# A recommender kernel's first chunk: first cross layer tile by tile in fp32, with the next tiles' attention groups between

## The chip, the cores and the metric

One core of one Trainium2 chip. The metric is the device time of one execution in microseconds (us). The kernel before took 2104.42 us, the median of three runs (2103.35 to 2104.58).

## What is computed

A recommender model for 2048 samples. Each sample has a target (an item embedding plus a projected image embedding), a history of 50 items, and two category fields.

```python
x = concat([t, seq_emb, t - seq_emb, t * seq_emb])          # 50 history items, 128 wide each
scores = (relu(x @ aw1 + ab1) @ aw2 + ab2)[..., 0]
weights = softmax(where(item_seq == 0, -1e9, scores))
hist_feat = einsum('bs,bsd->bd', weights, seq_emb)
sparse = stack([like_feat, view_feat, item_id_feat, item_img_feat, hist_feat])   # 5 x 128
se = sparse * w[:, :, None]                                  # gate from the fields' means
p = [vids[:, i] * se[:, j] for i in range(4) for j in range(i + 1, 5)]
dnn_in = concat([se, p])                                     # 15 x 128 = 1920
for i in range(2):
    xc = dnn_in * (xc @ cross_K[i] + cross_bias[i]) + xc
h = gelu(ln(xc @ w1 + b1)); h = gelu(ln(h @ w2 + b2)); return sigmoid(h @ w3 + b3)
```

## The kernel before

The samples are 16 tiles of 128, in four chunks of four tiles. Samples lie along the free axis in the cross layers: the 1920 features are 15 blocks (FEATS) of 128 partitions.

**A tile's attention** goes in five *groups* of ten history items. GpSimd gathers the items by indirect DMA (L445), ten a group and three more for a tile's features. For a group TensorE transposes the ten blocks (`transposes10`, L503; in the opening two halves, L496 and L509), ScalarE copies them to SBUF (`copy_eT10`), VectorE multiplies them by the target (`times_target`, L1116), TensorE computes the hidden layer (`hidden`, L528 and L532), VectorE takes the maximum (`hidden_max`, L1130), TensorE makes the scores (`score`, L539), VectorE does four small softmax operations (`softmax_max`, L1138 to L1144), ScalarE takes exponentials and weighs the ten blocks (`exps`, `weigh`, L829), and VectorE sums them (`history`, L1164 and L1167). Once a tile, VectorE prepares the target (`head_aim`, from L1093) and its negative (`head_neg`, L1108 and L1109), finishes the history and the gate (`tail_fold` from L1172, `tail_gate_apply`), and multiplies the pairs of fields (`tail_pairs`, L1199).

**The plan** (`make_plan`) sets the order by hand. A `Step` names what every engine issues in it: `grp` (transposes and `times_target`) at step k, `open` (`hidden`, `hidden_max`, `score`) at k + 1, `summed` (softmax, `weigh`, `history`) at k + 2. Each engine walks the same steps and takes its own part, in a fixed order. An opening of 28 steps prepares the first chunk's four tiles, with a group in nearly every step and no cross layer. A last group of its last tile is split (TAPER).

**A chunk** then is 30 steps, 15 output blocks in each of two cross layers, and a stage for `w1`. A step is three `products` calls of five feature blocks. Weights come from HBM into a ring of six (`raw`), and each is split into a high and a low part in fp32r (`w_hi` on ScalarE, `w_lo` on VectorE); activations likewise (`x_hi`, `x_lo`). Each block then takes three matmuls of 512 columns (L586 to L588). The attention groups of the next chunk's tiles lie inside these steps: groups at steps 1 to 5, 7 to 11, 13 to 17 and 19 to 23. In a step TensorE issues products 0, `hidden`, `transposes10`, products 1, products 2, `score`. VectorE's order in a step is, in short:

```python
if p.summed: softmax_max(*p.summed)
unit(c, 3 * k); if prev: x_scale(*prev)      # the previous output block
if p.open: hidden_max(p.open[0])
if p.summed: history(*p.summed)
unit(c, 3 * k + 1); if prev: x_lo(*prev)
if p.pair is not None: tail_pairs()
if p.grp: times_target(p.grp[0])
unit(c, 3 * k + 2)                           # then tail_gate_apply, tail_fold, head_aim
```

Two PSUM banks alternate between output blocks: products 0 of a step waits on `bank_free`, which VectorE gives after `x_scale` of the block before last. Loading the first `raw` blocks does not wait; later ones wait on `w_free`.

## Time and profile before

| | |
|---|---|
| median of the runs | 2104.42 us |
| profiled execution's own time | 2105.34 us |
| its span | 2103.0 us |
| PE / DVE / ACT / POOL busy | 92% / 64% / 43% / 43% |
| opening (to the first product of chunk 0) | 327.4 us |
| chunk 0, layer 0 | 327.4 to 539.4 us |
| moved by DMA | 220.27 MB |

The span is the time from the first to the last recorded instruction, and the execution's own time has 2.3 us more around it. A busy share of PE counts a matmul until its result has drained, so overlapping ones run closer together than their durations: the distance from one start to the next is what a matmul costs in a stream. An fp32 matmul shows as two records (x8 for four matmuls), a transpose or an fp32r matmul as one.

### The profile page before, as it was taken

To read this page: it belongs to the slowest core of one execution; us is meant where nothing else is said; L and a number is where in the kernel's file an instruction comes from. 1 tells how busy PE (TensorE), PEld (TensorE's weight loads), DVE (VectorE), ACT (ScalarE), POOL (GpSimd) and SP (SyncE) were. 2 spreads that over 40 slices of the span, in tenths; PEclk is the share of its full clock that TensorE was granted. 3 is DMA by queue.
4 is the path that set the end of the run, shared out by engine and by line. 5 is a ranking of instruction groups with operands and counts; after the bars stand their busy time and mean duration, and the time that the engine had idled before them with its cause. 6 is when DMAs were issued, how large, how long until landed. Compare 5 with 4: busy or idle time off the path is not lost. (4 is left out here: it accounts for less than half of the span.)

```text
span 2103.0 us, 32483 instructions
## 1 busy us (share of the span) xinstructions
PE 1936.4 (92%) x9608; PEld 1522.7 (72%) x9608; DVE 1337.0 (64%) x2248; ACT 903.0 (43%) x1927; POOL 893.9 (43%) x854
## 2 busy tenths in 40 slices
PE   1766658999999999999999999999999999999997
PEld 1444436778777887777777887777777888888886
DVE  4555555677778756667778755667778654445553
ACT  1443442545445244664544335654445243322234
POOL 7777777667566401657557302647550000000000
PEclk7666568999999999999999999999999999999998
DMA  5112113334344452334434452334432343333320
GB/s 164 50 49 53 48 52 98 104 111 137 115 121 121 137 174 79 96 90 142 117 111 132 129 182 71 100 96 140 116 106 88 116 167 126 93 96 97 98 68 1
DMA packets 99675, 220.27 MB, mean 105 GB/s; under 512 B 21792, under 2 KB 27184, under 8 KB 99376
## 3 DMA queue, kind: packets, MB, share of 16 engines
q1 hardware_dynamic: 63072, 136.90, 21.5%
q0 software_dynamic: 27136, 55.63, 10.4%
q10 hardware_dynamic: 9296, 25.70, 3.3%
q8 instruction: 79, 1.29, 0.3%
q14 instruction: 92, 0.75, 0.1%
HBM read 205.29 MB, written 12.85 MB: 104 GB/s over the span
## 5 line engine op out<-in xcount | busy, mean ns | idle before, releaser
L445 POOL DMA_INDIRECT e<-in_item_table,idx_all x800 | 843.7, 1055 | 649.4 <-POOLq L467 416.1
L870 ACT ACTIVATE Wh<-raw 128x640 fp32r<-128x640 f32 (+1 forms) x411 | 293.8, 723 | 508.9 <-ACTq L869 506.5
L1225 DVE TENSOR_TENSOR Wl<-raw,Wh 128x640 fp32r<-128x640 f32 (+1 forms) x411 | 331.9, 808 | 278.1 <-DVEq L1224 276.1
L586 PE MATMUL psum<-X0h,Wh 128*128 128x512 f32 x900 | 361.3, 401 | 1.3 <-PEq L584 1.3
L586 PE MATMUL psum<-X1h,Wh 128*128 128x512 f32 x900 | 357.1, 397 | 0.0
L587 PE MATMUL psum<-X0l,Wh 128*128 128x512 f32 x900 | 351.4, 390 | 0.0
L588 PE MATMUL psum<-X0h,Wl 128*128 128x512 f32 x900 | 351.1, 390 | 0.0
L587 PE MATMUL psum<-X1l,Wh 128*128 128x512 f32 x900 | 350.9, 390 | 0.0
L588 PE MATMUL psum<-X1h,Wl 128*128 128x512 f32 x900 | 350.4, 389 | 0.0
L829 ACT ACTIVATE e<-e,pw 128x128 f32<-128x128 f32 x800 | 242.8, 388 | 15.3 <-ACTq L142 15.3
L586 PEld LDWEIGHTS psum<-X0h,Wh 128*128 128x128 f32 x900 | 169.4, 188 | 36.5 <-issue 3.4
L588 PEld LDWEIGHTS psum<-X0h,Wl 128*128 128x128 f32 x900 | 169.1, 188 | 36.6
L588 PEld LDWEIGHTS psum<-X1h,Wl 128*128 128x128 f32 x900 | 169.0, 188 | 36.0
L586 PEld LDWEIGHTS psum<-X1h,Wh 128*128 128x128 f32 x900 | 169.1, 188 | 34.6 <-issue 1.0
L587 PEld LDWEIGHTS psum<-X1l,Wh 128*128 128x128 f32 x900 | 169.2, 188 | 32.8
L587 PEld LDWEIGHTS psum<-X0l,Wh 128*128 128x128 f32 x900 | 169.6, 188 | 32.1
L1164 DVE TENSOR_REDUCE hist<-e 128x128 f32<-128x1280 f32 (+1 forms) x65 | 156.6, 2408 | 52.9 <-DVEq L1162 52.9
L528 PE MATMUL psum<-eT,A 128*64 128x512 f32 (+2 forms) x640 | 138.5, 513 | 18.3 <-PEq L522 17.9
L1116 DVE TENSOR_TENSOR teT<-eT,tT 128x1280 f32<-128x1280 f32 x79 | 117.5, 1487 | 43.4 <-DVEq L1114 43.3
L539 PEld LDWEIGHTS psum<-cols,hidT 128*128 128x128 f32 x800 | 115.0, 217 | 35.5 <-issue 31.6
L539 PE MATMUL psum<-cols,hidT 128*128 128x2 f32 x800 | 110.2, 263 | 28.7 <-PEq L537 28.7
L532 PE MATMUL psum<-teT,A 128*64 128x512 f32 (+2 forms) x640 | 135.5, 503 | 0.0
(159 smaller groups left out, 2168.2 us busy)
## 6 DMA issues: line engine op xcount, KB each, us to landing
raw<-in_cross_K SPq DMA_DIRECT2D x360, 320.0 KB
raw<-in_w SPq DMA_DIRECT2D x51, 256.0 KB
e<-in_item_table,idx_all POOLq DMA_INDIRECT x800, 2.5
dnn_scratch<-dn ACTq DMA_DIRECT2D x12, 960.0 KB
x1f<-dnn_scratch ACTq DMA_DIRECT2D x3, 2048.0 KB, 9.8
x1f<-dnn_scratch ACTq DMA_DIRECT2D x3, 1792.0 KB, 15.6
e<-in_w SPq DMA_DIRECT2D x9, 256.0 KB, 4.8
dn<-in_embT SPq DMA_DIRECT2D x1, 1024.0 KB, 5.4
```

The costliest lines, as they stand in the source:

```text
L445: nc.gpsimd.indirect_dma_start(out=dst, out_offset=None, in_=table, in_offset=bass.IndirectOffsetOnAxis(ap=idx_all[:, t, s:s + 1], axis=0) ...
L528: last = mm(hsum[u * HID:(u + 1) * HID, a:b], A12[:], eT[:, u, a:b], start=True, stop=False)
L532: last = mm(hsum[u * HID:(u + 1) * HID, a:b], A3[:], teT[:, u, a:b], start=False, stop=True)
L539: last = mm(to[:, 2 * s:2 * s + 2], hidT[:, s * P:(s + 1) * P], col("aw2h", 0, 2), start=True, stop=True)
L586: m0 = mm(out, wh, Xh[:, 0:T, k, :], start=(k == 0), stop=False)
L587: m1 = mm(out, wh, Xl[:, 0:T, k, :], start=False, stop=False)
L588: m2 = mm(out, wl, Xh[:, 0:T, k, :], start=False, stop=(k == FEATS - 1))
L829: last = af(x, x, ACT.Copy, scale=pw[:, g % 2, s:s + 1])
L870: af(Wh[:, split_slot(w), 0:n], raw[:, rs, 0:n], ACT.Copy).then_inc(hi_done, 1)
L1116: v.tensor_tensor(teT[:].rearrange("p u (s b) -> p (u s) b", b=P), eT[:].rearrange("p u (s b) -> p (u s) b", b=P), tT[:, par:par + 1, :].t ...
L1164: done(v.tensor_reduce(hist[:] if g else acc[:, par, :], x, AX.X, ALU.add))
L1225: v.tensor_tensor(Wl[:, rs, 0:n], raw[:, rs, 0:n], Wh[:, slot, 0:n].bitcast(F32), ALU.subtract).then_inc(lo_done, 1)
```

## The change

Only chunk 0 and what leads up to it change. The opening now prepares one tile (OPEN = 1, 13 steps). Then come 45 *early* steps: three passes of 15 output blocks, one for each of tiles 0, 1 and 2, each computing layer 0 of its tile alone in plain fp32 (`solo_products`: one fp32 matmul of 128 columns for a block, no split of weights or activations). Tile 3's pass is the first 15 steps of chunk 0. In place of 675 fp32r matmuls of 512 columns there are 900 fp32 matmuls of 128 columns. Of the 15 output blocks' weights, those of even n (8 of them, 24 loads of 320 KB) are kept in SBUF (`kept`, where X1h and X0h lie later); the odd ones are streamed again in each pass. `solo_scale` is a VectorE operation on 128 x 128 in place of one on 128 x 512. TensorE waits for all kept blocks before the first pass.

The groups of tiles 1 to 4 are placed by SPREAD, counted from the end of the opening; tiles 5 to 7 come at steps 8, 14 and 20 and the four after each. The fields of tiles 0 to 3 are written straight into x0f, so that splitting them in the opening (`tail_hi`, `tail_lo`) goes, and in layer 1 of chunk 0 the sum X0h + X0l (`x_sum`) goes too. Blocks 0 to 13 of the first layer's result are split for layer 1 in pairs at steps 8 to 14 of tile 3's pass (HALVES). The first weight unit of layer 1 is split at step 14.

```diff
+OPEN = 1
+LAST = OPEN - 1
+PASSES = TILES[0] - 1
+KEPT = 8
+HALVES = {FULL + 2 + q: (2 * q, 2 * q + 1) for q in range(FEATS // 2)}
+SPREAD = ((-2, 0, 1, 3, 5), (8, 11, 14, 17, 20), (23, 26, 29, 32, 35), (38, 41, 44, 47, 50))
 GROUP_STEPS = {
     4: [[1 + 6 * j + g for g in range(NG)] for j in range(4)],
+    0: [[s + g for g in range(NG)] for s in (8, 14, 20)],
...
-    open_steps = lead + sum(len(groups(t)) for t in range(TILES[0])) + 4
+    open_steps = lead + sum(len(groups(t)) for t in range(OPEN)) + 4
+    early_steps = open_steps + PASSES * FEATS
+    plan += [Step(0, k, a) for a in range(PASSES) for k in range(FEATS)]
...
+            for b in range(KEPT * UNITS):
+                if b > 1:
+                    sp.wait_ge(kept_landed[b % 2], b // 2 * DMA)
+                n, kg = divmod(b, UNITS)
+                sp.dma_start(kept[:, n, kg * KG:(kg + 1) * KG, :].rearrange("p f b -> p (f b)"), kx_d[2 * n * UNITS + kg]).then_inc(kept_landed[b % 2], DMA)
...
+            def solo_products(a, n, kg):
+                out = xps[:, bank(a, n), 0:P]
+                if kg == 0:
+                    pe.wait_ge(bank_free, 1).then_inc(bank_free, -1)
...
+                    last = mm(out, block(i), x0f[:, a, k, :], start=(k == 0), stop=(k == FEATS - 1))
...
+            for i in range(2):
+                pe.wait_ge(kept_landed[i], KEPT * UNITS // 2 * DMA)
+            for p in early:
+                step(p)
...
+            def solo_scale(a, n):
+                dve.wait_ge(mm_done, 1).then_inc(mm_done, -1)
+                v.scalar_tensor_tensor(out=x1f[:, a, n, :], in0=xps[:, bank(a, n), 0:P], scalar=col("cb", n), in1=x0f[:, a, n, :],
+                                       op0=ALU.add, op1=ALU.mult).then_inc(scaled, 1)
...
+                if p.last:
+                    solo_scale(*p.last)
+                elif p.prev:
+                    x_scale(*p.prev)
```

VectorE before, at the end of layer 0 of chunk 0: from a group's softmax (L1138) in one step to the next group's `times_target` (L1116, output teT).

```order
L1138 SCALAR_TENSOR_TENSOR sc<-psum,tiny,keep 128x10 [waits score_ready]
L1141 TENSOR_TENSOR sc<-sc,mbias 128x10 [waits dve_done]
L1142 TENSOR_REDUCE tiny<-sc 128x1 [waits dve_done]
L1144 TENSOR_SCALAR nmax<-tiny 128x1 [waits dve_done]
L1225 TENSOR_TENSOR Wl<-raw,Wh 128x640 [waits hi_done]
L1253 SCALAR_TENSOR_TENSOR x1f<-psum,cols,x1f 128x4x128 [waits sum_done,mm_done]
L1130 TENSOR_TENSOR hidT<-psum,negT 128x640 [waits lo_done,scaled,h_ready]
L1149 COPY rsum<-gsum 128x1 [waits p_ready]
L1164 TENSOR_REDUCE acc<-e 128x128 [waits dve_done,weighed]
L1225 TENSOR_TENSOR Wl<-raw,Wh 128x640 [waits dve_done,hi_done]
L1271 TENSOR_TENSOR X1l<-x1f,X1h 128x4x128 [waits xhi_done]
L1116 TENSOR_TENSOR teT<-eT,tT 128x1280 [waits lo_done,eT_ready]
```

VectorE in the change, in the second pass over the spaced groups, from the softmax of one group (L1204) to `hidden_max` of the next (L1196); L1302 is `solo_scale`.

```order
L1204 SCALAR_TENSOR_TENSOR sc<-psum,tiny,keep 128x10 [waits score_ready]
L1207 TENSOR_TENSOR sc<-sc,mbias 128x10 [waits dve_done]
L1208 TENSOR_REDUCE tiny<-sc 128x1 [waits dve_done]
L1210 TENSOR_SCALAR nmax<-tiny,nmax 128x1 [waits dve_done]
L1302 SCALAR_TENSOR_TENSOR x1f<-psum,cols,x0f 128x128 [waits mm_done]
L1217 SCALAR_TENSOR_TENSOR rsum<-rsum,corr,gsum 128x1 [waits scaled,p_ready]
L1230 TENSOR_REDUCE hist<-e 128x128 [waits dve_done,weighed]
L1233 SCALAR_TENSOR_TENSOR acc<-acc,corr,hist 128x128 [waits dve_done]
L1302 SCALAR_TENSOR_TENSOR x1f<-psum,cols,x0f 128x128 [waits dve_done,mm_done]
L1182 TENSOR_TENSOR teT<-eT,tT 128x1280 [waits scaled,eT_ready]
L1302 SCALAR_TENSOR_TENSOR x1f<-psum,cols,x0f 128x128 [waits mm_done]
L1196 TENSOR_TENSOR hidT<-psum,negT 128x640 [waits scaled,h_ready]
```

Between the softmax and the next `times_target` the weight splits (Wl), the 512-wide scale and the activation split are gone; `history` (L1230, L1233) still stands ahead of `times_target` (L1182), now with three short steps where one long one was.

TensorE in the change, from the same group's `score` (L581) over one step of solo products (L633) to the transposes of the next group (L545). The `hidden` that waits on that next group's `times_target` comes 15 blocks later.

```order
L581 MATMUL psum<-cols,hidT 128x2 [waits hid_ready]
L581 MATMUL psum<-cols,hidT 128x2 x4
L633 MATMUL psum<-x0f,raw 128x128 [waits bank_free,raw_landed0]
L633 MATMUL psum<-x0f,raw 128x128 x4
L633 MATMUL psum<-x0f,raw 128x128 [waits raw_landed1]
L633 MATMUL psum<-x0f,raw 128x128 x4
L633 MATMUL psum<-x0f,raw 128x128 [waits raw_landed2]
L633 MATMUL psum<-x0f,raw 128x128 x4
L633 MATMUL psum<-x0f,kept 128x128 [waits bank_free]
L633 MATMUL psum<-x0f,kept 128x128 x4
L545 MATMUL psum<-ident,e 128x128 [waits tp_free,e_landed2]
L545 MATMUL psum<-ident,e 128x128 x9
```

Between a `score` and the next group's `hidden` lie 35 solo blocks of 128 columns and ten transposes. Before, where groups came in neighbouring steps, the next group's transposes and `times_target` were already issued ahead of a `score`, and one call of `products` (15 matmuls of 512 columns) lay between the `score` and the next `hidden`.

## Rows read from the trace of the kernel before

**Rows 1.** Stretches: us, busy time (x instructions) by engine, granted clock, DMA share, GB/s
```profile
46.70:327.40 280.70, 173.98 (x789) 117.88 (x789) 152.93 (x282) 113.83 (x320) 216.65 (x211) 0.63 0.19 51
327.40:539.40 212.00, 210.67 (x1111) 165.06 (x1111) 139.60 (x227) 94.44 (x206) 140.02 (x133) 1.00 0.41 116
```

**Rows 2.** Timeline, PE: start us, us, engine, line, op, tiles, shape, [idle before]
```profile
327.40 0.77 PE L586 MATMUL psum<-X0h,Wh 128*128 128x512 f32 x1
...
539.41 0.48 PE L586 MATMUL psum<-X1h,Wh 128*128 128x512 f32 x1
```

**Rows 3.** Groups by line, POOL, 46.7 to 327.4 us
```profile
L445 POOL DMA_INDIRECT e<-in_item_table,idx_all x199 | 205.0, 1030 | 60.7 <-issue 57.3 <-DMA e<-in_item_table,idx_all 3.4
```

**Rows 4.** Timeline, DVE, two opening steps at 101 to 112 us
```profile
101.19 0.35 DVE L1108 TENSOR_SCALAR negT<-psum,cols 128x128 f32<-128x128 f32 x1 [0.26 <-DVEq L1107]
102.26 0.23 DVE L1138 SCALAR_TENSOR_TENSOR sc<-psum,tiny,keep 128x10 f32<-128x10 f32 x1 [0.35 <-DVEq L1137]
...
104.24 1.48 DVE L1116 TENSOR_TENSOR teT<-eT,tT 128x1280 f32<-128x1280 f32 x1
...
110.60 0.35 DVE L1167 SCALAR_TENSOR_TENSOR acc<-acc,corr,hist 128x128 f32<-128x128 f32 x1 [0.24 <-DVEq L142]
111.21 0.23 DVE L1138 SCALAR_TENSOR_TENSOR sc<-psum,tiny,keep 128x10 f32<-128x10 f32 x1 [0.26 <-DVEq L1137]
```

**Rows 5.** Timeline, ACT, same steps
```profile
104.84 3.03 ACT L829 ACTIVATE e<-e,pw 128x128 f32<-128x128 f32 x10 [0.18 <-ACTq L142]
```

**Rows 6.** Timeline, PE, one group in chunk 0
```profile
400.32 1.08 PE L528 MATMUL psum<-eT,A 128*64 128x512 f32 x4
...
402.62 1.31 PE L503 MATMUL psum<-ident,e 128*128 128x128 f32 x10
403.69 0.49 PE L586 MATMUL psum<-X0h,Wh 128*128 128x512 f32 x1
...
410.64 1.17 PE L539 MATMUL psum<-cols,hidT 128*128 128x2 f32 x10
411.67 0.48 PE L586 MATMUL psum<-X0h,Wh 128*128 128x512 f32 x1
```

**Rows 7.** Timeline, PE, four full fp32 matmuls of 128 columns
```profile
647.80 1.16 PE L567 MATMUL psum<-dn,bil 128*128 128x128 f32 x8
```

**Rows 8.** Timeline, DVE, work done once a tile
```profile
120.08 0.48 DVE L1172 TENSOR_SCALAR S<-acc,tiny 128x128 f32<-128x128 f32 x1
...
122.14 0.17 DVE L1182 TENSOR_TENSOR tiny<-tiny,rows 128x5 f32<-128x5 f32 x1
...
553.38 0.29 DVE L1093 TENSOR_TENSOR tgt<-S 128x128 f32<-128x128 f32 x1 [0.32 <-DVEq L1235]
...
556.01 0.26 DVE L1103 TENSOR_SCALAR mbias<-idx_all 128x50 f32<-128x50 int32 x1
...
567.14 0.68 DVE L1271 TENSOR_TENSOR X0l<-x0f,X0h 128x512 fp32r<-128x512 f32 x1
567.75 1.67 DVE L1199 TENSOR_TENSOR dn<-dn,psum 128x512 f32<-128x512 f32 x4
```

**Rows 9.** Timeline, PE, two waits and what followed them
```profile
333.14 0.47 PE L586 MATMUL psum<-X0h,Wh 128*128 128x512 f32 x1 [1.33 <-PEq L584]
...
843.56 0.63 PE L658 MATMUL psum<-ident,dn 128*128 128x128 f32 x4 [2.80 <-PEq L656]
844.12 1.73 PE L528 MATMUL psum<-eT,A 128*64 128x512 f32 x4
...
848.12 1.31 PE L503 MATMUL psum<-ident,e 128*128 128x128 f32 x10
```

**Rows 10.** Timeline, DVE and PE, in the opening
```profile
76.80 0.29 DVE L1093 TENSOR_TENSOR tgt<-S 128x128 f32<-128x128 f32 x1 [0.32 <-DVEq L142]
...
311.79 0.22 DVE L1138 SCALAR_TENSOR_TENSOR sc<-psum,tiny,keep 128x4 f32<-128x4 f32 x1 [1.28 <-DVEq L1137]
...
323.03 1.30 PE L553 MATMUL psum<-ident,S 128*128 128x128 f32 x5 [11.39 <-PEq L551]
```

More of the change, by code:

```diff
@@ L88, with __init__ @@
 class Step:
-    def __init__(self, chunk, k):
+    def __init__(self, chunk, k, early=None):
         self.chunk, self.k = chunk, k
         self.layer, self.n = (None, None) if chunk is None else divmod(k, FEATS)
+        self.solo = early if early is not None else PASSES if chunk == 0 and self.layer == 0 else None
+        self.prev = self.last = None
+        if self.solo is not None:
+            self.last = (self.solo, self.n - 1) if self.n else (self.solo - 1, FEATS - 1) if self.solo else None
+        elif chunk is not None and (chunk, k) == (0, FEATS):
+            self.last = (PASSES, FEATS - 1)
+        elif chunk is not None:
+            self.prev = (chunk, self.layer, self.n - 1) if self.n else (chunk, 0, FEATS - 1) if self.layer else None
+        self.early = early is not None
+        self.split = ()
+        if chunk == 0 and not self.early and self.layer == 0:
+            self.split = HALVES.get(k, ())
+        elif self.prev:
+            self.split = (self.prev[2],)
+        elif (chunk, k) == (0, FEATS):
+            self.split = (FEATS - 1,)
         self.grp = self.open = self.summed = None
@@ L108, in make_plan @@
     where = []
-    for j in range(TILES[0]):
+    for j in range(OPEN):
         where.append([lead + NG * j + g for g in range(len(groups(j)))])
+    where += [[open_steps + k for k in ks] for ks in SPREAD]
     for c in range(1, CHUNKS):
-        at = open_steps + STEPS * (c - 1)
-        where += [[at + k for k in ks] for ks in GROUP_STEPS[TILES[c]]]
+        at = early_steps + STEPS * (c - 1)
+        where += [[at + k for k in ks] for ks in GROUP_STEPS[TILES[c] if c > 1 else 0]]
     for t, ks in enumerate(where):
@@ L294, in build @@
         raw_landed = [sem(f"raw_landed{i}") for i in range(WRING)]
+        kept_landed = [sem(f"kept_landed{i}") for i in range(2)]
         w_free = sem("w_free")
@@ L477, in _ @@
                 if t == LAST:
+                    pool.wait_ge(idx_in, DMA)
                     features(t + 1)
@@ L709, in step @@
                 T, k = p.fc, p.k
-                products(p.chunk, p.layer, p.n, 0)
+                products(p, 0)
                 if T and 2 <= k < T + 2:
@@ L715, in step @@
                 if p.pair is not None:
-                    tail_bilinear()
+                    tail_bilinear(p.pair)
                 if p.grp:
                     transposes10(*p.grp)
-                products(p.chunk, p.layer, p.n, 1)
+                products(p, 1)
                 if p.swing is not None:
@@ L728, in step @@
                     fc_w3(T)
-                products(p.chunk, p.layer, p.n, 2)
+                products(p, 2)
                 if T and 2 <= k < T + 2:
@@ L746, in _ @@
                 opening_step(p)
+            if opening[-1].open:
+                pe.wait_ge(hscore_free, 1).then_inc(hscore_free, -1)
+                score()
+            for i in range(2):
+                pe.wait_ge(kept_landed[i], KEPT * UNITS // 2 * DMA)
+            for p in early:
+                step(p)
             for c in range(CHUNKS):
@@ L979, in step @@
                     tail_copy(p.pair)
-                unit(c, 3 * k)
+                if not p.early:
+                    unit(c, 3 * k)
                 if p.fetch is not None:
@@ L985, in step @@
                     weigh(*p.summed)
-                if p.n or p.layer:
-                    x_hi(*((c, p.layer, p.n - 1) if p.n else (c, 0, FEATS - 1)))
+                for n in p.split:
+                    x_hi(c, p.prev[1] if p.prev else 0, n)
                 if p.grp:
@@ L1001, in step @@
                     fc_gelu2(pairs(T)[1])
-                unit(c, 3 * k + 2)
-                if p.pair is not None:
+                if not p.early:
+                    unit(c, 3 * k + 2)
+                if p.pair is not None and p.pair >= TILES[0]:
                     tail_store(p.pair)
@@ L1029, in _ @@
                 opening_step(p)
-                if p.k == 6:
-                    for w in range(LOOK):
-                        w_hi(w)
+            for p in early:
+                step(p)
             for c in range(CHUNKS):
@@ L1369, in step @@
                     head_neg(p.neg)
-                if prev:
-                    x_end(*prev)
+                if p.last:
+                    solo_end(*p.last)
+                elif p.prev:
+                    x_end(*p.prev)
                 if T and k == T + 2:
@@ L1455, in _ @@
                 opening_step(p)
-                if p.k == 6:
-                    for w in range(LOOK):
-                        w_lo(w)
-                        w_out()
+            for p in early:
+                step(p)
             for c in range(CHUNKS):
```

176 lines of the change are left out of this document (97 added, 79 removed).

## The prediction

> **What bounds the kernel now.** I read the stretches first. From 327.4 to 539.4 us TensorE is busy 210.67 of 212.00 us at full clock [rows 1]: layer 0 of chunk 0, between its first product and the first of layer 1 [rows 2], is bound by TensorE. From 46.7 to 327.4 us it is busy 173.98 of 280.70 us, with a mean granted clock of 0.63 [rows 1]. There the gathers set the pace: 199 take 205.0 us and 60.7 us between them, so 1.335 us each, 13.4 us for a group of ten, 70.8 us for a tile's 53 [rows 3]. So before chunk 0 some 190 us pass in which no cross product is made, and that is what the change tries to fill.
>
> The third thing to see is the chain of one group on VectorE and ScalarE. From the start of one softmax (102.26) to the next (111.21) 8.95 us pass: softmax, `hidden_max`, `times_target` and, after ScalarE's 3.03 us of weighing, `history` [rows 4, 5]. In the opening `times_target` stands ahead of `history` and fits into the wait for ScalarE. In a chunk's step it stands behind `history`, which costs nothing there, since a step lasts over 10 us.
>
> **What the change costs on TensorE.** A solo block is two fp32 records. Ten transposes take 1.07 us and ten records of `score` 1.03 us [rows 6], so a record costs about 0.107 us in a run and a block 0.215. The nearest row of full fp32 matmuls has four in 1.16 us with its drain, 0.29 each [rows 7]: that is the upper bound; I take 0.215, because passes are long runs. 900 blocks are then 194 us in place of 675 fp32r matmuls in 154 us (212.0 less twelve groups at 4.4 and some turns, so 0.228 each). A step is 15 blocks, 3.2 us, where it was over 10. A group adds 2.30 for `hidden`, 1.07 for the transposes, 1.03 for `score`, 4.4 in all [rows 6].
>
> **When the passes start.** Tile 0 runs as before until the aim of tile 1 at 76.80 [rows 10], which now comes three steps later, so the second softmax starts there. Three steps of 8.95 bring the fifth to 103.7; it, a short maximum and the aim (2.9, from 553.38 to 556.27 [rows 8]) bring the sixth to 108.7. From the last softmax (311.79) to the turn (323.03) it took 11.2 us [rows 10], so the turn is at 119.9. Behind it now stands tile 1's first group: turn 1.3, transposes 1.1 behind them, three copies about 2.5 (an estimate), `times_target` 1.48, `hidden` at the lower clock 4.0 (844.12 to 848.12 [rows 9]), four bilinear matmuls and a score at about 2 each. **Passes start at 135 us** in place of 327.4. The 24 kept loads are 7.9 MB, at 116 GB/s [rows 1] 68 us from about 10: hidden by the opening. Leaving out the splits of the fields saves only what stood before 327.4, which is counted with it.
>
> **The cycle of a spaced group.** In the passes a group comes every third step, and VectorE's order there is softmax, solo_scale, `history`, and only in the next step solo_scale and `times_target`, on which the next `hidden` waits. The chain is closed: 8.95 us from the softmax to past `history` [rows 4]; solo_scale with its handover 0.6 (the 128 x 128 operation at 110.60 takes 0.35 and the links 0.24); `times_target` 1.48 [rows 4]; handover 0.2; `hidden` 2.30; ten blocks 2.15; `score` 1.17 [rows 6]; handover 0.15. That is **17.0 us a group**. TensorE has 45 x 0.215 + 4.4 = 14.1 us of work in it, the gathers 13.4. So the chain ends last, and TensorE idles 2.9 us in each cycle, the larger piece before products 0 of the step of the next `hidden`, for `bank_free`, which solo_scale behind `history` gives. Spacing by three hides nothing: two steps would give the same 17.0.
>
> Once a tile this chain also takes the fold (120.08 to 122.31, 2.3), the aim (2.9), the pairs (1.67 and their wait, 2.0) [rows 8] and the negative (101.19 to 102.26, 1.0 [rows 4]): 8.2 us. A tile costs 5 x 17.0 + 8.2 = **93.2 us**, against 70.8 of gathers.
>
> **The sum**, to the first product of layer 1:
> - start of the passes, 135.
> - tile 1's other groups, to tile 2's first `times_target`: two groups in neighbouring steps with one chain each of 8.95, about 37 together with their hand-overs; then 17.0 and 17.0 + 3.3 (fold, negative): 74.5, so 209.5.
> - tiles 2, 3, 4: 3 x 93.2 = 279.6, so 489.1.
> - tile 5 in steps 8 to 12 of tile 3's pass, now with two activation splits (0.68 each [rows 8]): 8 to the next softmax, a step with aim and pairs of 16.9, two of 11.9, one of 10.3, then about 11 until the second weight unit of layer 1 is split, less the 3.4 us in which TensorE does the first: 67, so **556**.
>
> Against 539.4 [rows 2] layer 1 starts 16.8 us later. By then 31 groups are done where it were 32, so one more, 4.4 us, lies in layer 1, which TensorE bounds. The `x_sum` that goes is VectorE time beside a full TensorE, worth nothing. At full clock: +21.2.
>
> **The clock.** A wait of 1.33 us at 333.14 was followed by a stream at its usual distance; after a wait of 2.80 us at 843.56 `hidden` took 4.0 us in place of 2.30 [rows 6, 9], at 1.2 instead of 2.4 GHz for part of it. The waits of the passes, 2.2 us in one piece, lie between, and they stand right ahead of `hidden`, which is on the chain. So a cycle loses between 0 and 1.7 us; I take 0.7, in 18 cycles 12.6. The Trainium skill ("TensorE: Matmul & The Clock Gate", HAM oscillation) says that long idle gaps between bursts bring the lower clock back, and names only gaps longer than these; by it the passes would keep 2.4 GHz and this term would be nothing, 2126 us in all. The wait of 2.80 us speaks against it here, though barely.
>
> Sum: +33.8, on the profiled execution's own 2105.34 us 2139.1. The median lies 0.9 below that execution: **2138 us**, 1.6% slower.
>
> **Rivals.**
> - *The chain overlaps and TensorE is the bound* (the other side). Then layer 1 starts at 135 + 60 x 3.2 + 25 x 4.4 + about 10 = 447; the 331 gathers until then end at about 445, so both agree. 92 us earlier, less 4.4: 2017 us. For it: VectorE, at 139.60 of 212.00 busy, has room in total [rows 1]. Against it: the fixed order. It decides at a cycle of about 15.9 us at full clock; below, the change wins. One chain in between, at 15 us a cycle because handovers are shorter than mine and no clock is lost, gives about 2090. Chances 0.10 and 0.08.
> - *The clock stays up*: 2126. Chance 0.20.
> - *The clock stays at 1.2 GHz*, as in much of the opening (0.63 [rows 1]): a cycle has 28 us of TensorE's work, 18 cycles 200 us more, about 2320. Against: the passes are far denser than the opening. Chance 0.04.
> - *Kept loads disturb the opening*: they share the engines with the gathers and with the image stage ahead of 46.7 us, which nothing hides. 10 to 20 us on top of the forecast, 2148 to 2158. Chance 0.12.
> - Forecast: 0.46.
>
> **How the numbers follow.** Start (127 to 142), block price (up to 0.29, which puts 0.75 us on each of 18 cycles, 13 us) and clock (0 to 1.7 a cycle) put the forecast's own case within 2118 to 2165. The range 2092 to 2176 takes in the clock rival and the loads, and leaves out the overlap, half of the middle case, the cold clock and some tails, about 0.2. A measurement can tell 0.2% (4 us) from no change; the middle case crosses that band with 0.03. Faster 0.17, same 0.03, slower 0.80.
>
> **What would show it.** First solo product near 135 us; distance between one group's `history` and the next about 17 us in the second and third pass, with idle TensorE of about 3 us in each, ended by VectorE (bank_free, then te_ready); solo records 0.107 us apart; layer 1 of chunk 0 starting at 556 to 570; the stages behind it as long as before, but for one group. TensorE's idle ended by gathers instead, or cycles of 14 us, would prove me wrong.

## The result, and the profile after

The changed kernel takes 2137.8 us (median), the kernel before 2104.5: **1.57% slower**, a ratio of 1.0157 with an interval of 1.0139 to 1.0175. The profiled execution has 2138.24 us of its own and a span of 2136.4, 33.4 us more than the span before. The forecast was 2138.

The stretches come first, of the changed kernel and behind them the one of before that has no row yet (columns as in [rows 1]):

```profile
48.00:137.80 89.80, 49.79 (x239) 32.31 (x240) 41.97 (x89) 29.98 (x86) 65.88 (x66) 0.66 0.32 93
137.80:562.80 425.00, 355.11 (x2752) 308.56 (x2752) 198.13 (x390) 129.53 (x369) 260.12 (x252) 0.92 0.37 107
562.80:877.40 314.60, 307.54 (x1558) 243.80 (x1556) 217.91 (x357) 140.77 (x291) 147.64 (x138) 0.99 0.42 125
```

```profile
539.40:843.50 304.10, 301.00 (x1521) 239.94 (x1520) 216.41 (x356) 134.88 (x282) 121.67 (x115) 1.00 0.41 124
```

The opening ends at 137.8 us instead of 327.4 [rows 1]. In its place stand passes of 425.0 us in which TensorE is busy 355.1 us (84%) at a mean granted clock of 0.92; before, the 212.0 us of layer 0 had 210.7 us of TensorE's work at full clock. Layer 1 starts at 562.8 us instead of 539.4 [rows 2]: 23.4 of the 33.4 us. The other 10 arise behind it: the stretch up to the first turn of the next stage takes 314.6 us against 304.1, with TensorE 6.5 us more busy and 4.0 us more idle.

One cycle of a spaced group on VectorE (timeline: start in us, duration in us, and in brackets the idle time before it):

```profile
334.35 0.23 DVE L1204 SCALAR_TENSOR_TENSOR sc<-psum,tiny,keep 128x10 f32<-128x10 f32 x1 [2.62 <-DVEq L1203]
...
336.62 0.22 DVE L1217 SCALAR_TENSOR_TENSOR rsum<-rsum,corr,gsum 128x1 f32<-128x1 f32 x1 [0.68 <-DVEq L1213]
339.73 2.39 DVE L1230 TENSOR_REDUCE hist<-e 128x128 f32<-128x1280 f32 x1 [2.89 <-DVEq L1228]
342.36 0.35 DVE L1233 SCALAR_TENSOR_TENSOR acc<-acc,corr,hist 128x128 f32<-128x128 f32 x1 [0.24 <-DVEq L171]
342.97 0.35 DVE L1302 SCALAR_TENSOR_TENSOR x1f<-psum,cols,x0f 128x128 f32<-128x128 f32 x1 [0.26 <-DVEq L1301]
343.67 1.49 DVE L1182 TENSOR_TENSOR teT<-eT,tT 128x1280 f32<-128x1280 f32 x1 [0.35 <-DVEq L1180]
```

on ScalarE, whose weighing VectorE's 2.89 us of idle time wait for:

```profile
336.55 3.03 ACT L907 ACTIVATE e<-e,pw 128x128 f32<-128x128 f32 x10 [0.18 <-ACTq L171]
```

and on TensorE, of this cycle and of a later one:

```profile
334.06 3.59 PE L633 MATMUL psum<-x0f,raw 128*128 128x128 f32 x30
337.49 1.28 PE L633 MATMUL psum<-x0f,kept 128*128 128x128 f32 x10
338.61 1.25 PE L545 MATMUL psum<-ident,e 128*128 128x128 f32 x10
339.70 2.40 PE L633 MATMUL psum<-x0f,kept 128*128 128x128 f32 x20
343.77 1.35 PE L633 MATMUL psum<-x0f,kept 128*128 128x128 f32 x10 [1.67 <-PEq L632]
345.31 1.94 PE L570 MATMUL psum<-eT,A 128*64 128x512 f32 x4 [0.18 <-PEq L564]
346.98 1.96 PE L574 MATMUL psum<-teT,A 128*64 128x512 f32 x4
...
457.43 1.35 PE L633 MATMUL psum<-x0f,raw 128*128 128x128 f32 x10 [1.67 <-PEq L625]
458.96 1.08 PE L570 MATMUL psum<-eT,A 128*64 128x512 f32 x4 [0.18 <-PEq L564]
459.84 1.06 PE L574 MATMUL psum<-teT,A 128*64 128x512 f32 x4
...
477.29 2.48 PE L633 MATMUL psum<-x0f,kept 128*128 128x128 f32 x10 [4.62 <-PEq L617]
```

From softmax to softmax pass the weighing (3.03), the `history` reduce (2.39), `solo_scale` and only then `times_target`; TensorE has finished its products by 342.1 us and waits 1.67 us at the bank that `solo_scale` frees behind `history`. The same wait is followed at 345.31 by `hidden` with 1.94 us a run and at 458.96 with 1.08, the lower and the upper level of the clock. The last row is a cycle with the aim: its wait is 4.62 us and the ten records behind it, 2.48 us, are at the lower level.

The distances from one `times_target` (L1182) to the next in tiles 2 to 4 are 16.9 us (five of fifteen), 18.6 in one where the clock falls (behind 343.67), 18.6 to 19.3 for each tile's first, which has the pairs in it, 20.0 with the aim and 21.6 to 23.1 with fold and negative. From tile 2's first to tile 5's, 214.06 to 500.46 us, that is 286.4 us. In the stretch of 210 to 495 us TensorE's idle time is (groups by line):

```profile
L633 PE MATMUL psum<-x0f,kept 128*128 128x128 f32 x717 | 95.0, 288 | 23.0 <-PEq L617 17.9 <-PEq L632 5.1
L633 PE MATMUL psum<-x0f,raw 128*128 128x128 f32 x630 | 77.8, 278 | 6.5 <-PEq L625 6.5
L570 PE MATMUL psum<-eT,A 128*64 128x512 f32 (+1 forms) x120 | 25.9, 505 | 2.4 <-PEq L564 2.3
...
L588 PE MATMUL psum<-tT,A 128*128 128x128 f32 x6 | 2.0, 428 | 7.3 <-PEq L587 7.3
```

L617, L625 and L632 end waits ahead of the products: 29.5 us. L617 waits for the bank. L625 (a streamed weight block has landed) and L632 (the inputs are ready) stand directly behind it, so a wait for the bank shows at whichever of them comes last; that it is the bank's is settled by e2_short_sum below, where a shorter sum alone leaves three waits of 2.6 us of them in the same stretch, one a tile, all at L617. The 7.3 are the share of the target's preparation once a tile (L587). GpSimd's gathers end none of it: the transposes (L545), which wait for them, have no idle time.

### The profile page after: what moved, and what is told of

Read it like the earlier page. It is cut to its first block and busy times, and to the rows that moved or that the text cites. A ratio compares the mean times of both kernels' runs of the same rounds, so it can differ in the third digit from the quotient of the medians.

```text
span 2136.4 us, 34649 instructions
## 1 busy us (share of the span) xinstructions
PE 1961.3 (92%) x10733; PEld 1583.2 (74%) x10733; DVE 1284.1 (60%) x2213; ACT 860.4 (40%) x1863; POOL 890.7 (42%) x854
## 5 line engine op out<-in xcount | busy, mean ns | idle before, releaser
L1280 DVE TENSOR_TENSOR Wl<-raw,Wh 128x640 fp32r<-128x640 f32 (+1 forms) x366 | 294.9, 806 | 258.9 <-DVEq L1279 257.1
L658 PE MATMUL psum<-X0h,Wh 128*128 128x512 f32 x675 | 270.4, 401 | 0.0
L660 PE MATMUL psum<-X0h,Wl 128*128 128x512 f32 x675 | 263.2, 390 | 0.0
L659 PE MATMUL psum<-X0l,Wh 128*128 128x512 f32 x675 | 263.2, 390 | 0.0
L907 ACT ACTIVATE e<-e,pw 128x128 f32<-128x128 f32 x800 | 242.9, 388 | 15.7 <-ACTq L171 15.7
L1230 DVE TENSOR_REDUCE hist<-e 128x128 f32<-128x1280 f32 (+1 forms) x65 | 155.8, 2397 | 76.6 <-DVEq L1228 76.6
L633 PE MATMUL psum<-x0f,kept 128*128 128x128 f32 x960 | 128.0, 289 | 24.0 <-PEq L617 17.9
L660 PEld LDWEIGHTS psum<-X0h,Wl 128*128 128x128 f32 x675 | 126.7, 188 | 27.4
L658 PEld LDWEIGHTS psum<-X0h,Wh 128*128 128x128 f32 x675 | 126.9, 188 | 26.2 <-issue 1.4
L659 PEld LDWEIGHTS psum<-X0l,Wh 128*128 128x128 f32 x675 | 127.0, 188 | 24.2
L633 PEld LDWEIGHTS psum<-x0f,kept 128*128 128x128 f32 x960 | 119.7, 203 | 27.7 <-issue 27.7
L1196 DVE TENSOR_TENSOR hidT<-psum,negT 128x640 f32<-128x640 f32 (+1 forms) x81 | 66.1, 816 | 121.5 <-DVEq L1195 120.0
L1182 DVE TENSOR_TENSOR teT<-eT,tT 128x1280 f32<-128x1280 f32 x79 | 117.6, 1488 | 26.8 <-DVEq L1180 26.8
```

The source lines that it names most:

```text
L633: last = mm(out, block(i), x0f[:, a, k, :], start=(k == 0), stop=(k == FEATS - 1))
L658: m0 = mm(out, wh, Xh[:, 0:T, k, :], start=(k == 0), stop=False)
L659: m1 = mm(out, wh, Xl[:, 0:T, k, :], start=False, stop=False)
L660: m2 = mm(out, wl, Xh[:, 0:T, k, :], start=False, stop=(k == FEATS - 1))
L907: last = af(x, x, ACT.Copy, scale=pw[:, g % 2, s:s + 1])
L1182: v.tensor_tensor(teT[:].rearrange("p u (s b) -> p (u s) b", b=P), eT[:].rearrange("p u (s b) -> p (u s) b", b=P), tT[:, par:par + 1, :].t ...
```

## The experiments

Each diff is against the changed kernel unless it says otherwise. Single executions of a kernel spread more here than those of the kernel before (e1_late_history: 2106.5 to 2117.7 us), and the profiled one was often the fastest; so times are medians, and traces are compared with traces.

### Is VectorE's order the chain?

**e1_late_history**, the sum a step later for tiles 1 to 5, all groups but a tile's last (the lines of `make_plan` that fill `p.now` and `p.late` are left out here):

```diff
 # DVE, step()
-                if p.summed:
-                    history(*p.summed)
+                if p.now:
+                    history(*p.now)
...
                 if p.grp:
                     times_target(p.grp[0])
+                for q in p.late:
+                    history(*q)
```

> For tiles 1 to 5 the history sum of every group but a tile's last is done one step later, behind the next group's times_target; nothing else moves. Chain theory (the cycle of a spaced group, 16.9 to 18.6 us after, is set by VectorE waiting for ScalarE's weigh of about 3 us and then its own reduce of 2.4 us ahead of times_target, for which TensorE waits 1.67 us at a bank and 0.18 us at te_ready): the cycles of groups fall towards TensorE's own work, 15.0 us at full clock, and the dips of the clock that follow the waits go too; 4 distances a tile over four tiles, at 1.9 to 3.5 us each, are 30 to 56 us, so 2080 to 2108 us. Rival, TensorE's own work sets the cycle and the waits only move: the time stays within 5 us of 2138. Rival, the gathers set it: GpSimd's chain of 800 gathers at 1.05 us would hold a tile at about 52 us, which is below a tile's 88 us, so no change from this side.

Measured: 2115.9 us, ratio to the kernel before 1.0054 (1.0039 to 1.0069), so 22 us less than the changed kernel; profiled 2106.48 against 2138.24. The cycles are now 14.9 and 15.5 us, and tiles 2 to 4 take 251.3 us (207.12 to 458.46) instead of 286.4. Layer 1's first product comes at 522.1 us, 40.7 earlier. The chain theory holds, and the rival that TensorE's own work sets the 16.9 us falls, but the size was missed (2108 at most was expected): 9 of the 41 us are gone again in the trace's span (2104.6), see below.

**e1b_all_late**: the tile's last group too, with fold, gate and what follows one step later.

```diff
-        gate = last + 2 if t < OPEN else last + 3
-        plan[last + 2].fold = plan[gate].gate = plan[gate + 1].lift = plan[gate + 2].pair = t
+        gate = last + 2 if t < OPEN else last + (4 if t <= 5 else 3)
+        plan[gate if t < OPEN else gate - 1].fold = plan[gate].gate = plan[gate + 1].lift = plan[gate + 2].pair = t
```

> As e1_late_history, and the last group of each of tiles 1 to 5 too: all five history sums come one step later, behind times_target where there is one, and the tile's fold, gate, lift and pairs come one step later with it. Chain theory: 5 distances a tile instead of 4, so 5 to 10 us below e1_late_history, 2070 to 2100 us, unless the fold, one step later, meets the next tile's aim: then it is level with e1_late_history or up to 5 us above it. TensorE-bound rival: within 5 us of 2138.

Measured: 2127.4 us (1.0111, 1.0095 to 1.0128), 11.5 above e1_late_history, where 5 to 10 below or up to 5 above was expected. The next tile's first cycle is 21.6 to 21.9 us instead of 16.8: the fold has moved onto the chain of the tile behind it. A tile's last sum is worth more early.

**e2_short_sum**: the reduce of tiles 1 to 4 reads 2 of 10 rows and leaves out the other eight, all else in place.

```diff
-                x = e[:, first:first + 2 * n, :].rearrange("p s d -> p d s")
+                x = e[:, first:first + (2 if OPEN <= t <= 4 else 2 * n), :].rearrange("p s d -> p d s")
```

> For tiles 1 to 4 the history sum reads 2 of a group's 10 weighed rows (the other 8 are left out of the sum); ScalarE's weigh and every wait stay. The reduce falls from 2.39 us to about 0.5 us. Chain theory: about 20 cycles are each 1.7 to 2 us shorter at their end, and TensorE's wait of 1.67 us is nearly used up, so 30 to 40 us less, 2098 to 2108 us. Rival, VectorE's sum is hidden beside TensorE's work or the waits: within 5 us of 2138.

Measured: 2100.0 us (0.9978, 0.9969 to 0.9986), 37.8 less; the chain theory gave 30 to 40 less. VectorE's rows:

```profile
334.25 0.43 DVE L1230 TENSOR_REDUCE hist<-e 128x128 f32<-128x256 f32 x1 [2.88 <-DVEq L1228]
...
336.22 1.49 DVE L1182 TENSOR_TENSOR teT<-eT,tT 128x1280 f32<-128x1280 f32 x1 [0.35 <-DVEq L1180]
```

The reduce takes 0.43 us instead of 2.39, `times_target` starts 1.97 instead of 3.94 us after it, and the cycle falls from 16.9 to 15.0 us. It falls by 1.96 us at most, so the cycle alone doesn't say whether TensorE or still the chain sets 15.0. TensorE's rows of this run do: the last products before a `hidden` end at 322.78 us, and it starts 0.12 us later, with no wait marked in the whole cycle.

```profile
319.27 3.51 PE L633 MATMUL psum<-x0f,kept 128*128 128x128 f32 x30
322.90 1.08 PE L570 MATMUL psum<-eT,A 128*64 128x512 f32 x4
```

### How much room has TensorE?

**e3_filler** and **e3b_filler18**: in the passes' steps that sum a group, 9 or 18 extra matmuls ahead of the products.

```diff
+                    if k == 0:
+                        for _ in range(fill):
+                            mm(out, block(i), x0f[:, a, k, :], start=True, stop=True)
...
-                    solo_products(p.solo, p.n, kg)
+                    solo_products(p.solo, p.n, kg, FILL if p.early and p.summed and p.k + p.solo * FEATS > 7 else 0)
```

> In each step of the passes in which a group's history sum is done (after the first), the first column block's matmul is done nine times more, on the same operands and into the same bank, ahead of the products: 9 fp32 matmuls of two records at 0.112 us a record are 2.0 us of TensorE's time a cycle, in some 20 cycles. Chain theory (TensorE waits 1.67 us for the bank in these steps, for a chain of ScalarE and VectorE): most of the 2.0 us falls into the wait, so plus 0 to 12 us, and less than nothing if the filled wait also keeps the clock at its upper level: 2120 to 2150 us. Rival, TensorE's own work sets the cycle: plus 2.0 us in each of 20 cycles, 2175 to 2180 us.

> As e3_filler with 18 more matmuls instead of nine, 36 records at 0.112 us or 4.0 us a cycle. e3_filler took 2136.5 us against 2137.8 without any. Chain theory with a slack of about 2 us (1.67 us at the bank and 0.18 at te_ready): the first nine stay free and the other nine cost their 2.0 us in each of 13 to 20 cycles, less what the clock gives back by staying at its upper level: plus 15 to 40 us, 2150 to 2178 us. Rival, the wait is longer than it looks since the products behind it have slack too: under 2145 us.

Measured: with nine 2136.5 us (1.0158, 1.0143 to 1.0173), 1.2 us less than with none, which is no difference; with 18 2148.8 us (1.0216, 1.0201 to 1.0231), 11.1 more. Stretches of 210 to 305 us of the changed kernel, with nine, and with 18:

```profile
210.00:305.00 95.00, 82.14 (x663) 73.53 (x662) 41.63 (x84) 25.43 (x73) 55.83 (x54) 0.95 0.38 111
```

```profile
210.00:305.00 95.00, 91.36 (x753) 82.59 (x752) 40.99 (x83) 25.18 (x73) 55.15 (x54) 0.96 0.38 111
```

```profile
210.00:305.00 95.00, 93.62 (x804) 86.61 (x803) 39.39 (x75) 24.89 (x72) 50.43 (x51) 1.00 0.37 105
```

Nine matmuls, 2.0 us of work, change no cycle: 16.9 us again. With 18 the cycle is 18.9 us, TensorE is busy 93.6 of 95.0 us and the clock is 1.00. The 36 extra records take 4.1 us:

```profile
337.29 4.26 PE L636 MATMUL psum<-x0f,raw 128*128 128x128 f32 x36
341.39 3.51 PE L637 MATMUL psum<-x0f,raw 128*128 128x128 f32 x30
```

so TensorE's own work is 18.9 less 4.1, **14.8 us in a cycle**, and the slack in the changed kernel 16.9 less 14.8, 2.1 us. This is where the 14.9 us cycles of e1_late_history and the 15.0 of e2_short_sum stop as well: they are at TensorE's own work. The 15.5 us cycles of e1_late_history have one wait more, 0.34 us ahead of `score`, for `hidden_max`. That 18 cost 11 us, less than the 15 at least that was expected, has two reasons in the trace: cycles with the aim still take 20.0 us, since the wait there was 4.62 us, and those behind it take 20.0 instead of 21.6 to 21.9, since the clock no longer falls in the aim's wait (`hidden` at 291.32 us has 1.08 us a run, where the changed kernel has 1.98 at 288.87).

### Do the kept loads disturb the opening?

**e4_kept_later**: SyncE starts the kept loads behind the first `head_aim`.

```diff
+            sp.wait_ge(kept_go, 1)
             for b in range(KEPT * UNITS):
...
+                if t == 0:
+                    dve.sem_inc(kept_go, 1)
```

> SyncE starts the 24 loads of the kept blocks only behind VectorE's first head_aim (48 us), when the image stage has its rows. Theory (the kept loads take the DMA engines from the opening's image fetch, whose landing held VectorE 14.69 us against 10.20 before): the aim of tile 0 comes at about 43.8 us, the passes start 4 us earlier, and all that follows with them: 2132 to 2135 us. Rival, the loads, now from 44 to 95 us, take the engines from the gathers of tile 0 instead: no change or up to 5 us more, and the aim is early all the same. Rival, the 4.5 us have another cause: aim stays at 48 us.

VectorE's wait for the image rows, in the kernel before, the changed one and e4_kept_later:

```profile
43.78 0.29 DVE L1093 TENSOR_TENSOR tgt<-S 128x128 f32<-128x128 f32 x1 [10.20 <-DMA S<-img_scratch]
```

```profile
48.10 0.29 DVE L1159 TENSOR_TENSOR tgt<-S 128x128 f32<-128x128 f32 x1 [14.69 <-DMA S<-img_scratch]
```

```profile
43.67 0.29 DVE L1161 TENSOR_TENSOR tgt<-S 128x128 f32<-128x128 f32 x1 [10.22 <-DMA S<-img_scratch]
```

The DMA issues of 30 to 48 us (KB each, median us to landing), in the kernel before and the changed one; e4_kept_later has the first row again:

```profile
img_scratch<-dn ACTq DMA_DIRECT2D x1, 1024.0 KB, 4.6
```

```profile
kept<-in_cross_K SPq DMA_DIRECT2D x9, 320.0 KB, 4.4
img_scratch<-dn ACTq DMA_DIRECT2D x1, 1024.0 KB, 8.0
```

The cause of the late aim is shown: the store of the image's rows lands after 8.0 us instead of 4.6 beside nine kept loads, and without them the aim is back at 43.67. The passes start at 133.74 instead of 137.82 us, and in this one trace layer 1 starts at 556.4 instead of 562.8. The median is 2136.3 us (1.0157, 1.0144 to 1.0170), where 2132 to 2135 was expected: 1.5 us less than the changed kernel, less than the spread of either; that the 4 us reach the end is not shown.

**e4b_late_both**: both edits and a third. A late sum stays in its own step, behind `times_target`, when another group starts in that step, and comes one step late otherwise: `plan[k + 2 if plan[k + 2].grp else k + 3].late`, in place of `plan[k + 3].late`.

> e1_late_history and e4_kept_later together, the history sums at most one step late (two where the next group is two steps on). If the two are independent: 4 us below e1_late_history's 2115.9, 2110 to 2113 us. If tile 5's gathers bound e1_late_history from about 460 us on (GpSimd issued them back to back, 0.94 us and 0.30 us apart, from 499 us, and layer 1 waited 5.38 us at one product): an earlier start of the passes is eaten there and the time is 2114 to 2118 us.

Measured: 2106.2 us (1.0015, 1.0006 to 1.0023), 9.7 below e1_late_history, more than the 4 expected at most. In the traces only 3.4 us stand between the two spans (2101.2 and 2104.6), and layer 1 starts at 522.0 in one and 522.1 in the other. What gives the rest of the medians, and which of the two edits it comes from, is open. It is the fastest version here that computes all; it is still 0.15% above the kernel before.

### Where does the gain of the late sums go?

In e4b_late_both the last `times_target` of tile 4 comes 47.0 us earlier than in the changed kernel (430.40 against 477.35), that of tile 5 45.9 (500.92 against 546.83), layer 1 40.8 us, and the span ends 35.2 us earlier. I took GpSimd's gathers for the cause of the loss. Three runs on that have a fault of mine: they give tile 5's first group the same step as tile 4's last, so that **this last group of tile 4 is left out of the attention sums** (78 `times_target` of full size instead of 79). The step numbers of tile 5 in their expectations are three too high as well: a pass has 15 steps, so the changed kernel has tile 5 at 53 to 57.

```diff
 # e5b_even_kept, against e4b_late_both, without tile 5's late sums, as the next two
-SPREAD = (..., (8, 11, 14, 17, 20), (23, 26, 29, 32, 35), (38, 41, 44, 47, 50))
+SPREAD = (..., (8, 10, 13, 15, 18), (21, 23, 26, 28, 31), (34, 36, 39, 41, 44))
-    0: [[s + g for g in range(NG)] for s in (8, 14, 20)],
+    0: [[-1, 1, 4, 6, 9], [14, 15, 16, 17, 18], [20, 21, 22, 23, 24]],
 # e6b_tile5_apart_now: SPREAD as it was, tile 5 at [5, 7, 9, 10, 12]
 # e7_t1_apart: as e6b, tiles 1 to 3 at (-2, 0, 2, 4, 6), (9, 12, 15, 18, 21), (24, 27, 30, 33, 35)
```

> As e4b_late_both, and the groups of tiles 2 to 5 spread evenly over the passes: two and three steps apart in turn (tile 4 ends at step 44 instead of 50, tile 5 at steps 47 to 57 instead of 56 to 60); tile 5's history sums stay where they are in the changed kernel. Theory that e1_late_history lost 8 to 18 of its 41 us to late gathers, since GpSimd idles in the passes and tile 5's five groups stand one step apart there: the waits at 480 to 547 us go, and the time falls 6 to 15 us below e4b_late_both, to 2096 to 2106 us. Rival, groups two steps apart are bound by VectorE and ScalarE (a group's chain of weigh, reduce and times_target is 7 us and more against 7.2 us of products): the waits come back in the passes and the time stays at or above e4b_late_both's.

> As e4b_late_both, with tile 5's groups at steps 53, 55, 57, 58 and 60 of the first chunk's steps instead of 56 to 60, its history sums at their old place. In e4b_late_both TensorE waited 4.90, 2.03, 2.49, 3.18, 2.71 and 5.42 us between 476 and 546 us, and a group of gathers is about 12.5 us of GpSimd's time. Theory, these waits are for gathers that groups a step apart (8 us of TensorE's work each) ask for too fast: spread over eight steps they shrink by half or more, 5 to 12 us less than 2106, 2094 to 2101 us. Rival, a VectorE chain of about 14.3 us a cycle for groups two steps apart (e5b_even_kept had 14.3 to 14.9 us there, with TensorE waiting 2.80 us at te_ready): the waits only move, 2104 to 2112 us.

> As e6b_tile5_apart_now, and tile 1's groups at steps -2, 0, 2, 4, 6 instead of -2, 0, 1, 3, 5, tile 2's and 3's one step later. TensorE waits 2.3 to 2.8 us before four of the groups there. Theory, these are the chain of groups less than three steps apart: each step more of products takes 3.6 us of the wait: 2 to 4 us below e6b_tile5_apart_now. Rival, the work is only moved and the denser end of tile 3 (30, 33, 35) gives it back: within 2 us of it.

Measured: 2122.4, 2100.5 and 2106.1 us (one of the six executions of e5b_even_kept took 6869 us; why is open). As times of the kernel they count for nothing, since a group's work is missing. The last two leave out the same group: spacing tile 1's groups further made it 5.6 us slower, where 2 to 4 less or no change was expected. One thing more can be read in e5b_even_kept's trace, from groups that are all there: two steps apart with late sums, the cycles are 14.4 and 14.9 us and TensorE waits 2.80 us at `te_ready` (332.70 us). With two steps it has one step's 3.4 us less to do, so there the chain, and no longer TensorE, sets 14.4 us.

**e9_apart** and **e9b_apart_late5** repeat the thought, diffed against e4b_late_both, with nothing left out:

```diff
-SPREAD = (..., (8, 11, 14, 17, 20), (23, 26, 29, 32, 35), (38, 41, 44, 47, 50))
+SPREAD = (..., (8, 11, 14, 17, 19), (22, 25, 28, 31, 33), (36, 39, 42, 45, 47))
-    0: [[s + g for g in range(NG)] for s in (8, 14, 20)],
+    0: [[5, 7, 9, 10, 12], [14, 15, 16, 17, 18], [20, 21, 22, 23, 24]],
 # late sums for tiles 1 to 4 (e9_apart) or 1 to 5 (e9b_apart_late5)
```

> e5b_even_kept, e6b_tile5_apart_now and e7_t1_apart put tile 5's first group at the step of tile 4's last one, so that this last group was left out of the sums (their traces have 78 te products and 730 transposes, the changed kernel's 79 and 740): they can't be read as versions of the kernel. Here nothing is left out. Groups of tile 2 at steps 8, 11, 14, 17, 19, tile 3 at 22 to 33, tile 4 at 36 to 47, tile 5 at 50, 52, 54, 55, 57 (53 to 57 before); all else as e4b_late_both, with tile 5's history sums at their old place. Theory of gathers asked for too fast by tile 5's five groups in a row: part of e4b_late_both's 21 us of waits between 476 and 546 us goes, 2 to 8 us less than 2106, 2098 to 2104 us. Rival, the cycle of groups closer than three steps is 14 to 16 us whatever the products: the waits only come earlier, 2103 to 2110 us. The missing group was worth about one group's work and waits, 5 to 15 us, which e6b_tile5_apart_now's 2100.5 us already contain.

> As e9_apart, and tile 5's history sums behind the next times_target too, as in e4b_late_both. Chain theory: tile 5's cycles, two steps apart, lose VectorE's wait for weigh and its reduce ahead of times_target: 2 to 5 us below e9_apart. Gathers as the bound there: within 2 us of e9_apart, since a later sum also frees the gather's buffer later.

Measured: 2125.6 us (1.0105, 1.0090 to 1.0119) and 2112.1 us (1.0037, 1.0024 to 1.0051). e9_apart is 19.4 us over e4b_late_both, where neither theory had more than 4, but it changes two things: the spacing, and tile 5's sums, which stand at their old place. e9b_apart_late5 parts them. The late sums of tile 5 are worth 13.5 us, far more than the 2 to 5 expected: its first two distances are 14.4 and 15.4 us instead of 17.9 and 19.7. The spacing costs the other 5.9 us, where the gather theory had 2 to 8 us less: the gather theory falls. Part of these 5.9 stands in tiles 2 to 4, which gave up a step each: from tile 2's first `times_target` to tile 5's first they take 255.9 us instead of 251.5. TensorE's rows of the second group, e9_apart and then e9b_apart_late5:

```profile
496.45 1.97 PE L584 MATMUL psum<-eT,A 128*64 128x512 f32 x4 [5.89 <-PEq L578]
```

```profile
489.66 1.98 PE L584 MATMUL psum<-eT,A 128*64 128x512 f32 x4 [3.86 <-PEq L578]
```

In e4b_late_both itself GpSimd waits for a free buffer 16.06 us ahead of 477.58, while TensorE's long wait has VectorE's aim ahead of it. GpSimd, VectorE and TensorE:

```profile
477.58 0.95 POOL L502 DMA_INDIRECT e<-in_item_table,idx_all  x1 [16.06 <-POOLq L522]
```

```profile
476.91 0.29 DVE L1173 TENSOR_TENSOR tgt<-S 128x128 f32<-128x128 f32 x1 [0.31 <-DVEq L183]
...
480.38 0.23 DVE L1221 SCALAR_TENSOR_TENSOR sc<-psum,tiny,keep 128x10 f32<-128x10 f32 x1 [0.26 <-DVEq L1220]
```

```profile
480.91 0.70 PE L584 MATMUL psum<-eT,A 128*64 128x128 f32 x4 [4.90 <-PEq L582]
...
545.59 0.77 PE L672 MATMUL psum<-X1h,Wh 128*128 128x512 f32 x1 [5.42 <-PEq L670]
```

L582 waits for the scores' bank, which the softmax at 480.38 frees, and that softmax stands behind the aim. Between tile 5's neighbouring groups the distances are 8.7 to 15.7 us, while a step's products take 3.4 us: the same chain, closed over one step. From tile 5's first `times_target` to its last these are 48.1 us, and 46.4 in the changed kernel, so only 1.7 us are lost there.

The 5.42 us at 545.59 are the wait for the last of the 15 activation blocks that layer 1 reads (L670). VectorE and, in the second block, ScalarE:

```profile
526.75 1.48 DVE L1199 TENSOR_TENSOR teT<-eT,tT 128x1280 f32<-128x1280 f32 x1
...
528.62 2.37 DVE L1247 TENSOR_REDUCE hist<-e 128x128 f32<-128x1280 f32 x1 [0.26 <-DVEq L1245]
...
532.63 2.42 DVE L1247 TENSOR_REDUCE hist<-e 128x128 f32<-128x1280 f32 x1 [0.26 <-DVEq L1245]
...
540.15 0.34 DVE L1319 SCALAR_TENSOR_TENSOR x1f<-psum,cols,x0f 128x128 f32<-128x128 f32 x1
...
544.76 0.68 DVE L1357 TENSOR_TENSOR X1l<-x1f,X1h 128x512 fp32r<-128x512 f32 x1
```

```profile
540.86 0.63 ACT L977 ACTIVATE X1h<-x1f 128x512 fp32r<-128x512 f32 x1 [14.95 <-ACTq L975]
...
543.14 1.36 ACT L952 ACTIVATE Wh<-raw 128x640 fp32r<-128x640 f32 x2
```

The block is scaled at 540.15, its high part is made at 540.86, for which ScalarE had waited 14.95 us, and its low part at 544.76, behind a weight split that waits for ScalarE's of 543.14. The scaling is late because two late sums of tile 5, 528.15 to 535.6 us, stand ahead of it: from this `times_target` to the scaling 13.4 us pass, and 5.6 in the changed kernel (568.73 to 574.37), which has no wait of over 1 us at that place. So what moved out of the passes' chain stands in the way once at their end. That is read from the rows of two kernels; no run moved these two sums alone.

## Why the prediction was right

The sign, the size and the main mechanism held. That the number agrees to within 1 us is luck: terms missed by 2 to 7 us each, in both directions, and cancelled (2.8 at the start, 1.7 in tile 1, 3.7 less in tiles 2 to 4, 6.7 less in tile 5, about 6 more behind).

- **The cycle of a spaced group, 17.0 us at full clock**: measured 16.9. That the chain through VectorE's sum sets it, and not TensorE or the gathers, is shown from three sides: the sum behind `times_target` (14.9 to 15.5 us), a shorter sum (15.0), and work that TensorE takes on for nothing (16.9 with 2.0 us more). ScalarE's share, the 3.03 us of weighing that VectorE waits for, is read from the rows and was not varied.
- **TensorE's work in a cycle, 14.1 us**: measured 14.8, since a record costs 0.112 to 0.114 us (30 from 334.06 to 337.49, ten to 338.61) where 0.107 was taken, and the pieces have their edges. So TensorE idles 2.1 us a cycle (1.67 and 0.18 of it in the rows) and not 2.9. The upper bound of 0.29 a record was far off; the long run was the row to go by.
- **The clock, 0 to 1.7 us a cycle, 0.7 taken, 12.6 us in all**: too much, and put at the wrong place. Of twelve runs of `hidden` in tiles 2 to 4 that stand behind a short wait or none, one fell to the lower level (1.7 us); of the three behind the aim's 4.62 us all did, at 1.6 and 1.9 us in tiles 2 and 3 (21.6 and 21.9 against the 20.0 of e3b_filler18) and at most 3.1 in tile 4. That makes 5 to 8 us. The rival of a clock that stays up is refuted by the rows, and was near in size. The Trainium skill ("TensorE: Matmul & The Clock Gate", HAM oscillation) names only gaps longer than the short ones here: on the aim's wait the trace agrees, and in eleven of twelve short ones; the row at 345.31 stands against it. The same page has another section ("A second HAM failure mode: psum-queue depth-cycling"), which says that frequent very short idle times between groups of matmuls bring the lower clock too; the prediction overlooked it. By it the short waits would let the clock fall as well, and the trace agrees in that one case of twelve.
- **Start of the passes, 135**: 137.8. The missed part is the rival of the kept loads, which had 10 to 20 us and had 4.1 in e4_kept_later (137.82 to 133.74): I had called them hidden by the opening, looking at the gathers, and the image stage stood before those.
- **Up to tile 2's first `times_target`, 209.5**: 214.1, of which 2.8 are the start. **Tiles 2 to 4, 279.6 and 10.5 for the clock** (0.7 in 15 of the 18 cycles): 286.4, so 3.7 less; the clock's 5 to 8 us in place of 10.5 account for it within their bounds. **Tile 5 up to layer 1, 67 and 2 for the clock**: 62.3, some 7 less; which piece of the 67 was too long was not taken apart. Layer 1 at 562.8, where 556 and the clock's 12.6 gave 568.6.
- **Behind layer 1's start, one more group, 4.4 us**: 10.0 to 10.5. The group's own work was right; left out of the term were a wait and a lower clock. TensorE waits 3.94 us ahead of tile 6's first `hidden`, for a `times_target` (568.73 us on VectorE) that stands behind `history` and three splits, and this `hidden` takes 4.0 us (570.41 to 574.41) instead of 2.30. The 4.4, the 3.9 and these 1.7 are 10.0. The kernel before has no wait over 0.4 us from 539.4 us up to its 2.80 at 843.56. That this group brings the wait with it because it slipped into layer 1 is likely, but it was not tried. TensorE's rows:

```profile
570.41 1.77 PE L570 MATMUL psum<-eT,A 128*64 128x512 f32 x4 [3.94 <-PEq L564]
571.90 1.99 PE L574 MATMUL psum<-teT,A 128*64 128x512 f32 x4
...
574.41 1.31 PE L545 MATMUL psum<-ident,e 128*128 128x128 f32 x10
```

- **Two steps would give the same 17.0**: not measured clean. Tile 5's groups two steps apart in e9_apart had 17.9 and 19.7 us, with splits of X1 on the chain and the lower clock.
- **The rival on the other side**, TensorE as the bound, was to decide at a cycle of about 15.9 us. e2_short_sum has 15.0 and is 0.22% faster than the kernel before; e4b_late_both has 14.9 and 15.5 and is 0.15% slower. So the break-even lies at about 15 us and not 15.9; the middle case, 15 us a cycle, was priced at 2090 and gives 2100 to 2106. The other side's 2017 us could not be had by opening the chain alone: it gave TensorE 312 us between the first solo product and layer 1 (447 less 135), and in e2_short_sum TensorE is busy 346.1 of the 386.7 us there. That is 34 us more than the 312, and 40.6 us of idle time stand beside it, 10.8 in tile 1, 18.0 in tiles 2 to 4 and 11.8 in tile 5.

So why does filling 190 us without cross products not pay? The opening is 189.6 us shorter, and what stands in its place is 213.0 us longer. Of these, 144.4 us are TensorE's: 48 for the products (900 blocks at the measured 0.224, which is 202 us, in place of 154 by the forecast's count), about 57 for 13 more groups at 4.4 (an estimate), the rest once-a-tile work and the lower clock. And TensorE idles 69.9 us where it idled 1.3. The sum in the chain alone is worth 38 us of the time, by e2_short_sum. e4b_late_both takes most of that away (31.6 us of the medians), and arrives at about the old time.

## What to carry to other kernels

When work is moved from a place where each step lasts over 10 us to one where it lasts 3.4, the order of instructions on the helping engines must be looked at anew: a sum that cost nothing ahead of the next group's `times_target` became a part of the closed chain. Add up the whole loop from one softmax to the next and compare it with the bound engine's own work, before asking how busy each engine is; here TensorE was busy 84% of the passes and VectorE 47% (198.13 of 425.00), and the loop still set the pace. An extra load of that engine with useless work is a cheap measure of its slack, and the load at which the cycle grows gives its own work as well. A sum that is moved back to open the loop must still have a place at the loop's end: in e4b_late_both two of them stand ahead of the last block's scaling, and TensorE waits 5.42 us there.

A table of steps written by hand should be read back as the order of groups that it makes: a step given to two groups dropped one here, and the time looked like a gain.

## What the runs showed of the hardware

- Short waits (1.67 us at a bank and 0.18 behind it) were nearly always followed by the upper clock, 1.08 us for four matmuls of 512 columns, but once in one execution by the lower, 1.94; waits of 4.62 us by the lower in all three cases. Of three waits between them, 2.49 and 2.71 us in e4b_late_both and 2.70 in the changed kernel, one was followed by 1.98 us a run, one by 1.08 and one by 1.51.
- Useless matmuls in the waits were free (2.0 us in each cycle, 2136.5 against 2137.8 us in all). Twice as many brought the granted clock of 210 to 305 us from 0.95 to 1.00, and 11.1 us more of time.
- A 1 MB store took 8.0 us to land beside loads of 320 KB in flight on another queue, and 4.6 without them.
- The reduce over 10 rows of 128 takes 2.39 us and over 2 rows 0.43, near to proportion.
